# First expert fed and last expert returned by one-hot products in SBUF; bias products and key loads moved

## The reference

```python
gate_scores = jax.nn.softmax(xf @ Wg + bg, axis=-1)
top1 = jnp.argmax(gate_scores, axis=-1)
mask = jax.nn.one_hot(top1, num_experts, dtype=gate_scores.dtype)
masked = gate_scores * mask
gate = masked / (masked.sum(axis=0, keepdims=True) + EPS) * T
for e in range(num_experts):
    h = jax.nn.relu(jnp.einsum('bnd,dh->bnh', x, W1[e]))
    out = out + gate[..., e:e + 1] * jnp.einsum('bnh,hd->bnd', h, W2[e])
```

## Time and profile before

| | us |
|---|---|
| median of 3 runs | 1039.27 (1036.08 to 1044.47) |
| profiled execution, its time | 1038.23 |
| profiled execution, span | 1036.5 |
| PE busy | 956.8 (92% of the span) |
| DVE busy | 751.7 (73%) |
| ACT busy | 510.6 (49%) |
| POOL busy | 290.2 (28%) |
| mean granted PE clock | 0.974 |

### The profile page before, as it was taken

One profiled execution on the slowest core, in us unless ns is written; L12 is line 12 of the kernel. 1 busy time (PEld: TensorE's weight loads), 2 busy tenths in 40 slices (PEclk: granted clock), 3 DMA queues, 4 the chain that ended last, 5 costly groups with the idle time before them and its releaser, 6 DMA issues.

```text
span 1036.5 us, 17348 instructions
## 1 busy us (share of the span) xinstructions
PE 956.8 (92%) x6488; PEld 552.0 (53%) x6488; DVE 751.7 (73%) x1125; ACT 510.6 (49%) x1028; POOL 290.2 (28%) x439
## 2 busy tenths in 40 slices
PE   8896987999999977999589999999999999899988
PEld 4333353444444454999244444445788788644446
DVE  4989878988988631454489888884664745689856
ACT  2671341587878820111018888886312212358863
POOL 3656711133343203002302433331500410013230
PEclk9999998999999977999899999999999999999999
DMA  6789922103320333995342232201254243110001
GB/s 208 251 275 308 365 63 70 43 25 117 127 86 25 100 86 116 315 380 192 104 153 48 56 98 79 68 4 43 87 193 147 82 142 106 28 46 14 8 1 41
DMA packets 79182, 121.81 MB, mean 118 GB/s; under 512 B 9733, under 2 KB 52904, under 8 KB 79090
## 3 DMA queue, kind: packets, MB, share of 16 engines
q1 hardware_dynamic: 59278, 79.29, 24.6%
q10 hardware_dynamic: 19044, 39.22, 10.7%
q0 software_dynamic: 768, 2.10, 0.6%
HBM read 92.10 MB, written 27.81 MB: 116 GB/s over the span
## 4 chain that ended last, share of the span: by engine, by line
PE 68%; DVE 17%; DMA 5%; ACT 3%; issue 3%; POOL 3%; ACTq 1%; SPq 0%; DVEq 0%; POOLq 0%
PE st_bank L1622 14%; PE value_bank L1636 13%; PE max_bank L1865 11%; PE max_bank L1598 7%; DVE arena L2385 7%; PE max_bank L1807 4%; PE st_bank L1795 3%; DMA kparts<-arena 3%; PE max_bank L1388 2%; PE st_bank L1865 2%; PE st_bank L1544 1%; PE max_bank L1696 1%; PE max_bank L1795 1%; PE st_bank L1652 1%; DVE xn L1988 1%
## 5 line engine op out<-in xcount | busy, mean ns | idle before, releaser
L2385 DVE TENSOR_REDUCE arena<-max_bank 128x2 f32<-128x1024 f32 x320 | 375.3, 1217 | 40.1 <-PE max_bank L1598 39.5
L1235 ACT ACTIVATE arena<-st_bank 128x512 f32<-128x512 f32 x622 | 326.7, 604 | 93.7 <-PE st_bank L1622 90.0
L1636 PE MATMUL value_bank<-arena,vaug 128*9 128x256 f32 (+2 forms) x2560 | 169.2, 382 | 0.5 <-ACT arena L1235 0.5
L1622 PE MATMUL st_bank<-g_a 64*128 64x512 f32 x462 | 150.4, 473 | 0.3 <-ACT arena L1235 0.3
L1865 PE MATMUL max_bank<-g_a,g_w 128*128 128x512 f32 x512 | 117.3, 390 | 1.1 <-POOL g_a L986 1.1
L1622 PEld LDWEIGHTS st_bank<-g_a 64*128 64x128 f32 x462 | 63.2, 183 | 90.5 <-ACT arena L1235 88.2
L1865 PEld LDWEIGHTS max_bank<-g_a,g_w 128*128 128x128 f32 x512 | 95.9, 188 | 21.9 <-POOL g_a L986 2.0
L1598 PE MATMUL max_bank<-g_a 64*128 64x512 f32 x480 | 91.4, 439 | 8.2 <-DVE arena L2385 7.5
L953 POOL COPY arena<-arena 8x32 f32<-8x32 f32 x160 | 34.6, 216 | 221.6 <-issue 110.3
L1636 PEld LDWEIGHTS value_bank<-arena,vaug 128*9 128x9 f32 (+2 forms) x2560 | 56.0, 92 | 74.5 <-ACT arena L1235 21.0
L1329 ACT ACTIVATE arena<-max_bank,arena 128x512 f32<-128x512 f32 x32 | 22.0, 688 | 91.7 <-PE max_bank L1865 91.7
(11 more groups left out here) (388 smaller groups left out, 1463.2 us busy)
## 6 DMA issues: line engine op xcount, KB each, us to landing
arena<-in_glu_w SPq DMA_DIRECT2D x39, 512.0 KB, 3.2
arena<-kv_table SPq DMA_DIRECT2D x11, 1024.0 KB, 7.9
ctxT<-in_glu_w ACTq DMA_DIRECT2D x22, 512.0 KB, 6.0
arena<-in_w SPq DMA_DIRECT2D x20, 512.0 KB, 6.1
kparts<-arena ACTq DMA_DIRECT2D x12, 512.0 KB, 5.2
arena<-in_w ACTq DMA_DIRECT2D x12, 512.0 KB, 3.3
xnT<-kv_table SPq DMA_DIRECT2D x5, 1024.0 KB, 8.3
g_a<-kparts SPq DMA_DIRECT2D x24, 192.0 KB
```

The costliest lines, as they stand in the source:

```text
L1235: act.activation(prob[sl % PROBS][:, hh, :], bank[k], ACT.Exp, scale=scale).then_inc(exp_ready, 1)
L1622: pe.matmul(ring_bank(*place), Kc[gi % KQ_BUFS][rows, kt * P:(kt + 1) * P], Qc[gi % KQ_BUFS][rows, :], start=True, stop=True).then_inc(st_ ...
L1636: ins = pe.matmul(bank[7][at:at + dh + 1, 0:D], vaug[l][:, b * KT + 2 * m + i, h0 + hh, :], tiles[:, a], start=(m == 0 and i == 0), stop=( ...
L2385: dve.tensor_reduce(mxh[gi % 2][:, qt:qt + QT + 1:QT, half], max_pair[(p + FIRST_PAIR[l]) % len(max_pair)], AX.X, ALU.max).then_inc(max_re ...
```

## The change

The first expert no longer takes its tokens from `slot_in`. DVE writes eight one-hot tiles `first_hots` (128 tokens x 176 slots) and PE multiplies the tiles of `xn` by them, straight into the transposed input `unit_inT[0]`. The rank is now worked out first (`place`, the slot without overflow), so that `slots_ready` counts twice. SP loads seven blocks instead of eight; the second expert's block is the one with a semaphore of its own, and its transposes now stand behind the first expert's down products. The last expert no longer goes through `slot_out`: `place` is turned on PE, DVE compares it with the last expert's slots into `turned_hots`, and `last_expert(b)` multiplies them by `unit_out` into banks 3 to 6, from which DVE adds to the gathered rows (one add for two tiles). POOL's gathers wait for the stores of seven experts. SP's key loads of attention 2 move behind that and wait for `gathered[0]`. The bias products move ahead of the second half of the logits, the bias rows ahead of the ranks. The fillers go from 44 to 7 before the experts and from 35 to 0 after them. The reduction of the scanned bits moves behind the seventh expert's scans, the sum and the flags ahead of the overflow branch on PE; `clear_sums` moves behind the adds. Overflow units use banks 2 and 0 to 1.

```diff
-CTX_HOLD, UNIT_HOLD = 14, 44
+CTX_HOLD, UNIT_HOLD = 14, 7
...
 SP:
-                for e in range(E_MOE):
-                    ld(unit_in[0:SUB, e], unit_rows(slot_in, e), unit_x[min(e, 1)])
+                for e in range(1, E_MOE):
+                    ld(unit_in[0:SUB, e], unit_rows(slot_in, e), unit_x[min(e - 1, 1)])
...
-                    sp.wait_ge(unit_y, e + 1)
-                    sp.dma_start(unit_rows(slot_out, e), unit_out[e % 2][0:SUB]).then_inc(unit_st[e % 2], 16)
-                keys_load(2, 0)
+                    if e < E_MOE - 1:
+                        sp.wait_ge(unit_y, e + 1)
+                        sp.dma_start(unit_rows(slot_out, e), unit_out[e % 2][0:SUB]).then_inc(unit_st[e % 2], 16)
...
+                keys_stored(2)
+                sp.wait_ge(gathered[0], 16 * QT)
+                for g in (*range(1, KQ_BUFS), 0):
+                    keys_load(2, g)
...
 PE:
-            ln_transposes(3, [1])
-            gate_logits(1)
             for l in (2, 3):
...
+            ln_transposes(3, [1])
+            gate_logits(1)
+            pe.wait_ge(prepv_evac, NCT + 1)
+            for l in (2, 3):
+                ins = pe.matmul(bank[3][:, (l - 2) * D:(l - 1) * D], onesf[0:1, :], w[l]["bo"][:], start=True, stop=True)
...
+            hold_clock(UNIT_HOLD, 2)
+            for t in range(NT):
+                pe.wait_ge(onehot_ready, 2 + t)
+                for c in range(DC):
+                    ins = pe.matmul(bank[c][:, 0:CAP], xn[:, t, c * P:(c + 1) * P], first_hots[:, t, :], start=(t == 0), stop=(t == NT - 1))
+            ins.then_inc(unit_tr, 1)
+            pe.wait_ge(slots_ready, 1)
+            for t in range(NT):
+                ins = pe.transpose(bank[6 + t // QT][0:SUB, t % QT * P:(t % QT + 1) * P], bc(place[:, t:t + 1], [P, SUB]), ident[:])
...
-            hold_clock(UNIT_HOLD, 2)
             for e in range(E_MOE):
-                if e == 0:
-                    pe.wait_ge(unit_x[0], 16)
-                    unit_transposes(0, unit_in[:, 0], unit_tr, unit_xT)
...
                 unit_down_products(e, e % MOE_BUFS, unit_hid, unit_down, unit_yT)
+                if e == 0:
+                    pe.wait_ge(gate_ready, 1)
+                    pe.wait_ge(onehot_ready, 1 + NT + B)
+                    pe.wait_ge(unit_x[0], 16)
+                    unit_transposes(1, unit_in[:, 1], unit_tr, unit_xT)
...
+            def last_expert(b):
+                for t in range(b * QT, (b + 1) * QT):
+                    for i in range(2):
+                        ins = pe.matmul(bank[3 + t // 2][:, t % 2 * D:(t % 2 + 1) * D], turned_hots[0:SUB, i, t * P:(t + 1) * P],
+                                        unit_out[(E_MOE - 1) % 2][0:SUB, i, :], start=(i == 0), stop=(i == 1))
+                    ins.then_inc(unit_turn, 1)
+
+            pe.wait_ge(unit_y, E_MOE)
+            last_expert(0)
+            pe.wait_ge(flag_ready, 3)
             pe.wait_ge(over_ready, 1)
...
-            hold_clock(LN_HOLDS[4], 2)
-            pe.wait_ge(gathered[0], 16 * QT)
-            hold_clock(GATHERED_HOLDS, 2)
+            last_expert(1)
             attention(2)
...
 DVE:
+            for t in range(NT):
+                dve.tensor_scalar(first_hots[:, t, :], row_f, place[:, t:t + 1], None, ALU.is_equal).then_inc(onehot_ready, 1)
...
+            dve.wait_ge(unit_tr, 1)
+            dve.tensor_copy(unit_inT[0], st_bank[:, 0:DC, 0:CAP]).then_inc(unit_xT, 1)
+            for c in range(B):
+                dve.wait_ge(rank_mm, 2 + c)
+                for i in range(2):
+                    ins = dve.tensor_scalar(turned_hots[0:SUB, i, c * CH:(c + 1) * CH], bank[6 + c][0:SUB, :], last_f[0:SUB, i:i + 1], None, ALU.is_equal)
...
+                    if e == E_MOE - 2:
+                        dve.wait_ge(scan_done, GLU_CHUNKS)
+                        ch.link(dve.tensor_scalar(scan_bits, scan_bits, BF16_REST, None, ALU.bitwise_and))
+                        dve.tensor_reduce(low_sum, scan_bits, AX.X, ALU.max).then_inc(sum_ready, 1)
...
             for t in range(NT):
-                dve.wait_ge(gathered[t // QT], 16 * QT)
+                if t % 2 == 0:
+                    dve.wait_ge(gathered[t // QT], 16 * QT)
+                    dve.wait_ge(unit_turn, E_MOE + t + 2)
+                    ch.link(dve.tensor_tensor(xn[:, t:t + 2, :], xn[:, t:t + 2, :], bank[3 + t // 2].rearrange("p (j d) -> p j d", j=2), ALU.add))
```

More of the change, by code:

```diff
@@ L531, in build @@
         unit_outT = [r.take([DC, CAP]) for _ in range(2)]
+        hots_at = r.at
+        first_hots = r.take([NT, CAP])
+        assert r.at <= KQ_AT - 2 * D
+        r = Region(hots_at)
+        turned_hots = r.take([2, T])
         assert r.at <= KQ_AT - 2 * D
@@ L580, in build @@
         assert r.at <= end_l0
+        last_out = next(step for step in reversed(schedule(1)) if step[0] == "out")[2]
+        BIAS_BANK = TURN_BANKS[(last_out + 1) % 3]
         def context_sums(l, n):
@@ L1282, in _, with hidden @@
             ups = FM // UP_PER_BANK
-            def hidden(n, up, ready, down):
+            def hidden(n, up, ready, down, banks=4):
                 for i in range(ups):
@@ L2556, in _ @@
             scan(0)
-            copy_in(0, unit_tr, unit_xT, unit_up)
             for e in range(E_MOE + 1):
@@ L2596, in _ @@
                     normalise_batch(4, 0)
+            dve.wait_ge(unit_y, E_MOE)
+            clear_sums()
             second_queries()
```

130 lines of the change are left out of this document (66 added, 64 removed).

## The result

The changed kernel takes 1026.49 us, the median of four runs (1026.07 to 1027.27), beside 1038.80 for the kernel before in four runs of the same comparison (1036.08 to 1044.47). The ratio is 0.986, 95% interval 0.983 to 0.989: faster by 12.3 us where 18.3 were forecast. A second series, further down, gave 1024.29 and a ratio of 0.988 (0.984 to 0.993). The profiled execution took 1026.74 us with a span of 1025.0.

What follows compares the result with a forecast made beforehand. PE is 92% busy, so only its waits before and behind the experts can give much: 13.8 + 8.2 - 1.5 - 1.2 - 0.8 = 18.5 us gained. Forecast 1020.5 us, range 1013 to 1030.

Steps and rivals of the forecast that it cites:

- third and fourth rivals: Third: clock lost at both ends, 1034.8, chance 0.08; fourth: experts stay at low clock without fillers, 1049.5, chance 0.04.
- "right" ones: First up product 12 us earlier, second expert 13 to 14, gather before last down products end, L1394 some 20 earlier.
- "wrong" ones: PE waiting over 2 us for `slot_in`, clock 0.50 beyond first up products, PE idle on issue or DVE waiting at `last_expert`.
- the first expert: Ahead of the experts: one-hot feed starts the first up product at 395.0 instead of 407.33.
- the second expert's rows: New wait behind the first expert: rows land at 403.5, 1.6 before PE asks, or 405.2 if POOL's DMAs stretch.
- scatter and load follow `slot_i` as before ... 15.6: From slots ready to rows landed takes 15.6 us as before, so 387.9 gives 403.5.
- my 13.8: Second expert starts at 406.3 instead of 420.13: 13.8 us gained, bounds 11 to 16.4.
- theory A: For `later_and_keys`: Relus 1.2 us apart, second expert 34.3 to 34.9 behind the logits, last at 99.3, whole 1020 to 1022.
- the tail: Behind the experts: gather 8.2 us more gained, less 1.5 and 1.2 for DVE's adds and 0.8 for the clock.
- If it lands 2 late that is 2 lost: Tail: second half's gather beside key loads has until 492.7 to land, taken as hidden; 2 us lost if 2 late.

Runs made afterwards that it cites:

- the four kernels executed once: Changed kernel with one edit each: chunk loads an expert later, 1021.11 us; one scatter of eight, 1022.44; POOL's memset later, 1035.09; SP's registers read earlier, 1027.70.
- later_and_keys: Changed kernel with ACT's chunk loads and scans starting at the second expert, four an expert, and key loads behind the whole gather; 1024.01 us, ratio 0.984.
- one_scatter: Changed kernel without seven of the eight scatter DMAs, so later experts see mostly zero rows; 1022.44 us, executed once.
- registers_first: Changed kernel with SP reading its two overflow registers ahead of the seventh expert's store instead of behind it; 1027.70 us, executed once.
- pool_behind_mask: Changed kernel with POOL's memset of `g_x` waiting for the reduced bits instead of the last scan; 1035.09 us, executed once.

## Why the prediction was right, and where it was wrong

**Right: the place and the sign.** The wait for the first rows went and the return shrank (L1394 starts 24.5 behind the last expert instead of 30.5), nothing behind attention 2's start grew beyond the spread (513.4 us from the second row maximum on before, 514.7 after, and 513.1 to 514.9 in the others), and the period of the experts is 10.37 in the kernel after as before. The third and fourth rivals did not occur: the one-hot products ran at clock 1.00. But of the signs that I had set, three of the "right" ones failed (the second expert came 11.0 earlier, not 13 to 14, L1394 16.9, not some 20, and the gather started 0.1 behind the end of the last down products, not ahead of it), and of the "wrong" ones two showed: a clock of 0.50 beyond the first up products, and PE idle on issue between the halves of `last_expert`, though only for 1.18.

**Right, a little low: the first expert.** Forecast 12.3, measured 13.7. The bias products were hidden, the ranks came 2.4 earlier (forecast 2.3), and the first expert's up products ran at the full clock. Most of the rest lies behind the one-hot products, from whose end to the first up product it took 1.05 where I had put 1.9.

**Wrong: "the second expert's rows".** The step that failed is "scatter and load follow `slot_i` as before ... 15.6". The scatter did. The load did not: I took its 2.81 from a stretch in which nothing but the other experts' rows was loaded. I counted what the change moves on PE, DVE, POOL and SP, and not that ACT's three chunk loads hang on the Relus and move with them into the rows' landing, which becomes 6.0 to 7.6 where it is seen: the rows are there at +35.2 and +36.8, where 403.5 was +32.9. Behind it the clock falls, for another 1.6 to 2.3. Where the two don't meet the second expert starts at +34.3 to +34.6, 14.7 to 15.1 gained and more than my 13.8; as built it starts at +36.6 to +38.5, and the changed kernel's 38.35 gives 11.0. This is the term of 13.8 that measured 11.0: 2.8 of the 4.7 that are missing at the end of the span. That 11.0 is also the lower bound of my range for the term is luck: I had put it there for other reasons.

In the profiled execution it isn't that wait that shows, but ACT's stand, which costs a wait of 2.62 where the fronts without it have 0.55, and 1.65 on the down products, and hides the landing. The 2.8 missing in this execution are the stand's: less 2.07 and 1.65 the second expert would start at +34.6, if the rows were there. In executions without the stand the landing takes 2.0 to 4.2 at the same place. The stand alone gives +37.7 to +38.4, the landing alone +36.6 to +38.5: taking one away shows the other. Why ACT stands is open. It came in seven of twelve profiled executions with the one-hot front: in the changed kernel both times, in the three kernels with edits in the tail alone and in the two that hold the loads back, and in none of the four kernels executed once, of which two had the same front unchanged. `later_and_keys` was without it, which agrees with its theory A, but so were those two with their chunk loads in place. No instruction-fetch packets lie in the stretch. In all seven the second Relu comes 4.3 us behind the first and also 1.2 to 1.4 behind the end of the last up product, and in all seven PE's second signal is recorded only 0.02 before it, the third and fourth 0.1 later each.

Three things that the traces hold narrow it down. First, it goes with the series and not with the edit: of the profiles with the one-hot front the seven are all of three series and the five all of two others, of which one is that of the four kernels executed once. Second, the second Relu starts within 0.2 us of SP's issue of the rows' load, that is, when the last scatter has landed. Third, the traces of the seven lack records: of the 128 semaphore counts of the eight scatters they hold 32 to 44, those of the five hold all (128 of 128, and 16 of 16 in `one_scatter`). So the late signals may belong to the way in which these executions were recorded, and whether the executions without a profile have the stand is not shown.

**Right: the tail.** 4.7 forecast, 4.1 measured, term by term: gather 0.5 later behind the last expert (mask beside the memset), `last_expert` hidden on both sides of the branch, the first four query products 3.79 instead of 2.00, the adds at 0.69 each instead of 0.75. "If it lands 2 late that is 2 lost" was the right doubt and too large: DVE waited 0.59 for the second half, and in the second profile not at all.

**The sum.** 11.0 + 4.1 is 15.1 up to the first row maximum and 13.8 at the end of the span. The medians give 12.3 and 15.1 in the two series of the kernel; the start of the program differs by up to 9 us between executions, is no part of the change, and is larger than that difference. Of the 4.7 missing in the stages, 2.8 are the second expert's start, 0.6 the tail, and 1.3 lie behind it, inside the spread named above.

## What to carry to other kernels

When a step is moved forward, list also what *other* engines start at its end: a Relu's finish that issues three 512 KB loads takes them along. Take a landing time only from a row with the same company on the queues, or price it by both. And before holding a load back, look who waits for its data ahead of more urgent work in its own list. Loads and their users are best moved together, and even that had a price here, 2.4 and 3.5 us over the later experts. Last, profile the same kernel in several series before a stall is called its own.

## What the runs showed of the hardware

- A load of 176 KB landed in 2.81 us (`before`) with only its own kind beside it, and in 6.03 and 7.62 us (`registers_first`, `pool_behind_mask`) when three loads of 512 KB were issued 0.5 to 1.4 us before it.
- In seven profiles ACT idled 3.8 to 3.9 us between two Relus, PE's signals for the second, third and fourth being recorded within 0.23 us of each other, where the same products in other profiles signal 1.2 us apart. These seven traces also hold only 32 to 44 of the 128 semaphore counts of the scatters beside it. Not explained.
- A DVE `tensor_scalar` of 128x1024 (int32) takes 0.69 us alone and 1.52 us when a POOL memset of 0.96 us begins with it.
- PE's clock was 0.72 of full speed on average in the 6 us behind a stand of 2.6 us, and the 32 products from there on took 6.69 instead of 5.04.
- The first logits start between 370.0 and 378.9 us in 14 profiled executions of programs with the same beginning. Stages are to be compared from a common event, not from the start of the span.
